# Retention: who masks the second eight heads' scores

## The reference, cut to what matters

```
scores = einsum('bhld,bhmd->bhlm', q, k) * D[None]      # D[h, n, m] = gamma_h ** (n - m), 0 above the diagonal
ret    = einsum('bhlm,bhmd->bhld', scores, v)
ret    = (ret * silu(xo)) @ reto_w + reto_b
x      = x + ret
```

## Time and profile before

| | us |
|---|---|
| median of 3 runs | 1049.51 |
| lowest and highest | 1049.19, 1051.26 |
| profiled execution, its own time | 1046.18 |
| profiled execution, span of the trace | 1044.3 |
| DVE busy | 602.1 (58%) |
| ACT busy | 331.3 (32%) |
| POOL busy | 329.7 (32%) |
| PE busy | 702.2 (67%) |

### The profile page before, as it was taken

The page is one execution under the profiler, slowest core; times in us unless marked ns, Lnnn a source line. Parts: engine busy times, 40 slices in busy tenths (PEclk is TensorE's granted clock), DMA queues, the critical chain, the costliest instruction groups (busy, mean ns, idle before and its releaser), DMA issues. The chain is left out here.

```text
span 1044.3 us, 19748 instructions
## 1 busy us (share of the span) xinstructions
PE 702.2 (67%) x6652; PEld 477.3 (46%) x6652; DVE 602.1 (58%) x1825; ACT 331.3 (32%) x565; POOL 329.7 (32%) x654
## 2 busy tenths in 40 slices
PE   1789887889883119997215398378569863089991
PEld 0355455555562018996111144234234432078991
DVE  7978545889288706664504376246347527146763
ACT  2232324333421014442320156145245541034440
POOL 0123300134331756776430001101100115746771
PEclk9899998999975559999555599779779985589996
DMA  9101595111200115553321101101100000145554
GB/s 225 43 26 57 118 190 123 42 42 42 56 1 10 47 50 154 159 166 112 112 107 71 53 3 47 82 11 42 79 17 3 3 1 32 51 119 150 156 162 133
DMA packets 99569, 80.89 MB, mean 77 GB/s; under 512 B 7383, under 2 KB 91418, under 8 KB 98730
## 3 DMA queue, kind: packets, MB, share of 16 engines
q1 hardware_dynamic: 94926, 70.25, 24.9%
q0 software_dynamic: 4544, 9.38, 2.7%
HBM read 54.44 MB, written 23.40 MB: 75 GB/s over the span
## 5 line engine op out<-in xcount | busy, mean ns | idle before, releaser
L1153 DVE TENSOR_REDUCE rmax<-PA 128x1 f32<-128x512 f32 (+3 forms) x256 | 120.9, 490 | 151.1 <-PE PA L1791 143.3
L728 POOL DMA_INDIRECT outs_dram<-va,ids x78 | 93.8, 1202 | 54.8 <-POOL ids L724 27.8
L1086 DVE SCALAR_TENSOR_TENSOR pm<-PB,invb,decay 128x512 f32<-128x512 f32 x78 | 58.1, 744 | 61.9 <-ACT decay L1400 61.9
L1751 PE MATMUL PC<-ffn_w,pm 128*128 128x128 f32 x624 | 88.0, 284 | 6.9 <-DMA ffn_w<-in_w 4.8
L1789 PE MATMUL PA<-mqb,idb 128*128 128x128 bf16 x256 | 60.6, 238 | 45.1 <-DMA qst<-qst 29.9
L1791 PE MATMUL PA<-kst,qst 96*128 96x512 bf16 (+3 forms) x256 | 84.5, 336 | 0.0
L1751 PEld LDWEIGHTS PC<-ffn_w,pm 128*128 128x128 f32 x624 | 75.7, 191 | 11.1 <-DMA ffn_w<-in_w 7.2
L1392 ACT ACTIVATE kv_b<-P 128x256 f16<-128x256 f16 x78 | 29.9, 383 | 156.3 <-PE P L1730 152.2
L713 POOL DMA_INDIRECT rows_dram<-va,idx x64 | 64.4, 1006 | 45.7 <-DVE va L1039 26.8
L1467 ACT ACTIVATE pm<-PB 128x1024 f32<-128x1024 f32 (+1 forms) x64 | 44.9, 702 | 101.9 <-PE PB L1814 101.8
L1789 PEld LDWEIGHTS PA<-mqb,idb 128*128 128x128 bf16 x256 | 25.5, 100 | 107.6 <-issue 58.2
(11 more groups left out here) (214 smaller groups left out, 1585.4 us busy)
## 6 DMA issues: line engine op xcount, KB each, us to landing
ffn_w<-in_w SPq DMA_DIRECT2D x78, 256.0 KB
rows_dram<-wall SPq DMA_DIRECT2D x1, 8385.0 KB, 46.3
X<-in_w SPq DMA_DIRECT2D x32, 256.0 KB, 2.9
proj_w<-rows_dram SPq DMA_DIRECT2D x78, 65.0 KB
qst<-parts_dram SPq DMA_DIRECT2D x12, 384.0 KB
kst<-parts_dram SPq DMA_DIRECT2D x12, 384.0 KB
X<-in_x SPq DMA_DIRECT2D x8, 256.0 KB, 4.8
R<-outs_dram SPq DMA_DIRECT2D x4, 512.0 KB, 3.8
```

The costliest lines, as they stand in the source:

```text
L728: nc.gpsimd.indirect_dma_start(out=outs_dram, out_offset=bass.IndirectOffsetOnAxis(ap=ids[:, k % YB:k % YB + 1], axis=0), in_=ysb[:, k % Y ...
L1086: nc.vector.scalar_tensor_tensor(out=eT[:, k % 2, :, :].rearrange("p f n -> p (f n)"), in0=PB[:, k % 2, :], scalar=invb[:, k % 2:k % 2 + 1 ...
L1153: nc.vector.tensor_reduce(rmax[:, i, h % HG:h % HG + 1], PA[:, n % 2, 0:(i + 1) * P], AX_X, ALU.max).then_inc(pair_sb[n % 2], 1)
L1751: ins = mm(PC[:, k % 2, 0:D], eT[:, k % 2, f, :], w2b[k % WB2][:, f, :], start=f == 0, stop=f == FB - 1)
```

## The change

The masking of heads 8 to 15 is taken from VectorE and done in two steps. ScalarE copies the raw scores from PB into the second half of `pm` (`raw_scores`), and GpSimd multiplies them there, in place, with the decay (`decay_half`). Two semaphores are new, `raw_sb` and `pm2_sb`; `pm_sb` now counts one per tile. TensorE's next scores wait for VectorE's masking of PA and for ScalarE's copy; its retention product waits for VectorE and for GpSimd. On ScalarE the four copies of a group stand between the other work: one before the Silu, one behind it, and one behind each of the two high halves' places. On GpSimd the product stands behind `decay_k` and ahead of `norm_factors`.

```
+            def decay_half(g):
+                pool.wait_ge(raw_sb, g + 1)
+                nc.gpsimd.tensor_tensor(pm[:, 2 * (g % 2) + 1, :], pm[:, 2 * (g % 2) + 1, :],
+                                        decay[:, H // 2:H, :].rearrange("p h n -> p (h n)"),
+                                        ALU.mult).then_inc(pm2_sb, 1)
...
+            pool.wait_ge(in_decay, 16)
             for layer in range(LAYERS):
                 for t in range(NT):
                     decay_k(layer * NT + t)
+                    decay_half(layer * NT + t)
                     if t % TPS == 2 and t > TPS:
                         norm_factors(layer * SEQ + t // TPS - 1)
...
-                        decay_scores(t, 0)
+                        decay_scores(t)
                     if t >= 2:
                         add_out(t - 2)
-                    if t < NT:
-                        decay_scores(t, 1)
...
+                def raw_scores(t):
+                    g = layer * NT + t
+                    act.wait_ge(sc_ps, 2 * g + 2)
+                    if g >= 2:
+                        act.wait_ge(re_ps, g - 1)
+                    nc.scalar.activation(pm[:, 2 * (g % 2) + 1, :], PB[:, :, :].rearrange("p b n -> p (b n)"),
+                                         ACT.Copy).then_inc(raw_sb, 1)
...
+                    raw_scores(TPS * s)
                     nc.scalar.activation(sxT[:, c % 2, :], ring("xo", layer, s), ACT.Silu,
                                          bias=proj_bc[:, layer, 3:4]).then_inc(ring_sb, 1)
+                    raw_scores(TPS * s + 1)
                     if layer == 1:
                         high_weight(2 * s)
+                    raw_scores(TPS * s + 2)
+                    if layer == 1:
                         high_weight(2 * s + 1)
+                    raw_scores(TPS * s + 3)
                     if s >= 1:
                         normalize(2 + 2 * layer, s - 1)
...
                     if g >= 1:
-                        pe.wait_ge(pm_sb, 2 * g)
+                        pe.wait_ge(pm_sb, g)
+                        pe.wait_ge(raw_sb, g)
...
-                    pe.wait_ge(pm_sb, 2 * g + 2)
+                    pe.wait_ge(pm_sb, g + 1)
+                    pe.wait_ge(pm2_sb, g + 1)
```

More of the change, by code:

```diff
@@ L429, in mixer_kernel @@
         pm_sb = sem("pm_sb")
+        raw_sb = sem("raw_sb")
+        pm2_sb = sem("pm2_sb")
         re_ps = sem("re_ps")
@@ L867, in decay_q, with decay_scores @@
                         bc(const[:, C_GQ:C_GQ + P], [P, TPS, P], 1), ALU.mult).then_inc(qg_sb, 1)
-                def decay_scores(t, u):
+                def decay_scores(t):
                     g = layer * NT + t
[L871 to L875, removed]
+                    dve.wait_ge(sc_ps, 2 * g + 1)
+                    nc.vector.tensor_tensor(pm[:, 2 * (g % 2), :], PA[:, :, :].rearrange("p b n -> p (b n)"),
+                                            decay[:, 0:H // 2, :].rearrange("p h n -> p (h n)"),
                                             ALU.mult).then_inc(pm_sb, 1)
@@ L1702, in down @@
                     ins.then_inc(f2_ps, 1)
-                pe.wait_ge(pm_sb, 2 * NT * (layer + 1))
+                pe.wait_ge(pm2_sb, NT * (layer + 1))
                 pe.wait_ge(ro_up, NT * (layer + 1))
```

## The result

The changed kernel takes 1064.12 us (median of 4 runs, 1058.39 to 1065.81); the kernel before 1050.38 in its own 4. One of those four took 1125.42 us, in a slower state that the chip is sometimes in, and the ratio leaves it out; the other three have a median of 1049.51. The ratio is 1.0125, 95% interval 1.0079 to 1.0172: slower by some 13 us. The forecast was 1064.3. It stood at 315.2 us before and stands at 329.2: +13.9. (The whole span is longer by only 12.3; where the last 1.6 came back was not examined.)

What follows compares the result with a forecast made beforehand. VectorE, or TensorE, sets the pace, with GpSimd's chain on the path entering tiles 8 and 12. Layers' +4.7 and +10.1 us make 1046.18 into 1061.0; 3.3 for the runs' median gives 1064.3, range 1053 to 1072 (8 in 10).

Steps and rivals of the forecast that it cites:

- the hold: In both retention stages, VectorE instructions with two SBUF operands (state updates, decay_q, layer 1's low_weight) wait behind GpSimd's 2.36 us product.
- The walk: All engine queues followed tile by tile through both retention stages: +4.7 us in layer 0, +10.1 in layer 1, +14.8 in sum.
- the port: GpSimd instructions and VectorE ones with two SBUF inputs exclude each other; the walk without this gave +5.0 us.
- the late chain: At the entry to tiles 8 and 12, GpSimd's product delays norm factors, normalising, evacuation and TensorE's projections; alone +5.0 us.
- rival 1: No mutual holding of GpSimd and VectorE, only the chain late: +1.9 and +3.1 us, 1052 to 1054.5; chance 0.12.
- Layer 0, tiles 0 to 5, +0.7: Tile 0's retention product waits for GpSimd, which ends 2.5 us later than VectorE's second half did: +0.7 us.
- Entry to tile 12, "+2.36 again": Layer 0: tile 10's product again precedes the chain, +2.36 us; VectorE having won back 1 us, lateness is +3.5.
- Rival 3: TensorE's clock also falls behind the idle gaps before tiles 8 and 12 in each layer: +6.8 us, 1071; chance 0.10.
- Layer 0 should lose half of what layer 1 loses: Sign across the two layers: forecast +4.7 and +10.1 us; equal losses would say the weights' halves have no part.
- If the time from tile 4 to tile 8 is not 24 to 26 us in both layers, the walk is wrong: Sign to check the walk: time between the maskings in tiles 4 and 8, expected 24 to 26 us in both layers.
- Rival 2: TensorE becomes the bound and VectorE's relief shows; the four groups shrink by up to 7 us: 1042.5; chance 0.06.
- rival 4: The change moves nothing because TensorE's work covers both: within 2 us of 1049.5; chance 0.04.

Runs made afterwards that it cites:

- both layers filled: The changed kernel with small idle TensorE products before the fourth group's query projection and the last retention in each layer; 1.0040 of the kernel before.
- norm factors first: The kernel before, with GpSimd's norm factors moved ahead of decay_k in tiles 6, 10 and 14; 0.9985 of the kernel before.
- The fills: The changed kernel with GpSimd's product replaced by three scratch fills, together as long, reading nothing from SBUF; 1.0093 of the kernel before.
- the layer 1 run: The changed kernel with small idle products filling TensorE's gaps in layer 1 only; 1.0075 of the kernel before, the change beside it 1.0113.
- the hybrid: The changed kernel with ScalarE and GpSimd masking only in each group's first two tiles, VectorE in the others; 1046.45 us, 0.9932 of the kernel before.
- the copy-only kernel: The changed kernel with ScalarE's copy kept but VectorE, not GpSimd, multiplying the copied scores in SBUF; 1.0022 of the kernel before.
- half the product: The changed kernel with GpSimd's product covering 512 of 1024 numbers, four heads keeping raw scores; 0.9973 of the kernel before.

## Why the prediction was right, and where it was wrong

The sign was right, and so were the durations, the places of the waits and the hold as such. That the number was right to 0.2 us is luck: the forecast put the hold too high by some 6 us and the clock at nothing, where it is 6 to 8.

**Durations, places, the hold: right.** The product at 2.36 us and not 2.13; the copy at 1.02; no table load; `decay_k`, product, norm factors, normalising, evacuation, projections in that order, with a gap of 3.40 us for "3 to 4". The norm factors of tile 6 end at 74.2, not 75.6, since the product could start at 67.2 and not 68.65. A held state update of 2.23 us and low halves up to 2.2 (I had said up to 3). The estimate of 2.25 from the Trainium skill (GPSIMD Engine Reference, "Elementwise — side-by-side cycle accounting") was 5% low against the trace's 2.357; the figure of that page is for an add, where I had written product.

**The walk against the profiles.** Lateness in us against the kernel before, counted in each layer from its first masking:

| | forecast | the change | both layers filled |
|---|---|---|---|
| layer 0, tile 4 | +0.7 | -0.8 | 0.0 |
| layer 0, tile 8 | +2.2 | +2.5 | +1.7 |
| layer 0, tile 12 | +3.5 | +2.1 | +2.5 |
| layer 0, last sum | +4.7 | +2.1 | +1.4 |
| layer 1, tile 8 | +3.6 | +3.6 | +2.2 |
| layer 1, tile 13 | +6.0 | +3.8 | +3.7 |
| layer 1, last sum | +10.1 | +9.9 | +7.1 |

The last column is nearest to the waits alone, which is what the forecast added up. Its sum at the FFN end is +7.7. The kernel before has a half-speed stretch, some 1.6 us by the run with its norm factors first, and the filled kernel one of 0.8; with both taken off the waits are 7.7 + 1.6 - 0.8 = 8.5 us, where the forecast had 14.8.

**The step that was sized wrong: what the hold costs.** The prediction's own walk without the port gave +5.0, so 14.8 holds 9.8 us for the hold. The fills, without it, are 3.0 us faster than the change by the ratios, and about 4 earlier at the FFN end by the estimate above. Taken off 8.5 that leaves some 5 us for the late chain alone, an estimate, as rival 1 had it. So the hold was put too high by about 6 us, and the chain about right. In the table it shows most in the second half of layer 1, where the low halves of the weights are held: from tile 8 to the last sum the filled kernel loses 4.9 us, where I had 10.1 - 3.6 = 6.5, and tile 13 stands at +3.7 for +6.0. Why a held instruction costs less there than walked was not tested.

**Layer 0, tiles 0 to 5, +0.7: wrong sign.** The rows of the change show why.

```profile
38.73 1.21 DVE L883 TENSOR_TENSOR pm<-PA,decay 128x1024 f32<-128x1024 f32 x1
39.87 0.41 DVE L867 TENSOR_TENSOR vs<-PC,kv_b 128x256 f32<-128x256 f32 x1
41.22 1.23 DVE L883 TENSOR_TENSOR pm<-PA,decay 128x1024 f32<-128x1024 f32 x1 [0.94 <-PE PB L1631]
```

Tile 1's masking comes 2.5 us behind tile 0's; it was 3.65 before, when TensorE waited for VectorE's second masking before it could start tile 1's scores:

```profile
41.04 0.70 PE L1610 MATMUL PA<-kst,qkp 32*128 32x512 f32 x2 [1.66 <-DVE pm L873]
```

The wait that the prediction named is there, tile 0's retention product stands idle for 1.01 us until GpSimd is done, but VectorE's relief is worth more. (In the change's first profile tile 4 of layer 1 is also earlier, by 0.5 us; in the two later ones it is 0.1 and 0.3 later.)

**Entry to tile 12, "+2.36 again": no new wait.** TensorE has no gap of 0.9 us or more there in either layer, and between tiles 8 and 12 the change loses nothing.

**Rival 3, the clock: it got 0.10 and 6.8 us, and it was there.** Measured are 6.2 to 7.7 us by the filled gaps, and 7 to 8.5 with the filled kernel's own slow stretch taken off. Two of the four gaps are those that it named, in front of tile 8; tile 12 has none, and the other two are in front of each layer's last retention. Against it I had put that the fall of before stands where TensorE is busy without a break, but TensorE had been idle for 1.25 us just ahead of it, until 109.17; and that a slow stretch would lie partly in the idle time, but it came behind, when TensorE worked. So rival 3's mechanism held, while its total of 1071 failed, for the waits under it were smaller. That the parts add up to the measured +13.9 to +15.5 (8.5, and 7 to 8.5 for the clock, less 1.6 for the stretch of before) is so by construction; the independent check is the layer 1 run, 4.4 us of them with one layer filled.

**"Layer 0 should lose half of what layer 1 loses":** from the first masking of a layer to the last sum it lost 2.1 and 9.9 us, a fifth. The slow stretch of before lay in layer 0, and the low halves in layer 1; with both layers filled and that stretch added back it is 3.0 and 7.1, nearer to half. **"If the time from tile 4 to tile 8 is not 24 to 26 us in both layers, the walk is wrong":** it was 26.1 and 26.9, so by its own sign the walk was wrong. With the gaps filled it is 24.5 and 25.2: what it lacked there is the clock.

**Rivals 1, 2 and 4** fell by their totals; of rival 1 the price of the late chain fits. Rival 2 has a core of truth, which the hybrid shows: relief of VectorE is worth a few us (7 by the ratio) as soon as GpSimd isn't on the path.

## What to carry to other kernels

An engine that is busy a quarter of the time may still have no slack at a certain place in its queue. Before work is moved to it, find where others wait for it, and put the work where they don't: half of the moved products made this kernel faster, all of them slower. A wait that opens a gap of some 3 us on TensorE may cost twice, in the gap and in the clock behind it; filling the gap with idle products is a cheap test of which it is. And a total that comes out right doesn't show that its terms are: compare the walk with the profile place by place.

## What the runs showed of the hardware

In the change's three profiles each of the four gaps of TensorE of 2.8 to 3.4 us went with half speed (it begins within 1.5 us of the gap's end, behind it or just ahead); products in the gap, 2.84 us of them in front of tile 8, prevented it. No length of gap tells by itself whether the clock falls. Of the gaps of 0.9 to 1.3 us inside the layers of the change's first profile one was followed by half speed, the 1.21 us until 253.84 (0.72 over 254 to 260), and the others weren't; in the copy-only kernel all three of 1.37 us were (0.51 over 68 to 71, 0.50 over 92 to 95, 0.57 over 112 to 115); in half the product those of 2.25 and 2.44 us were, and in the hybrid one of 0.88.

A GpSimd product of 2.36 us holds a state update on VectorE to its end, 2.23 us instead of 0.34; GpSimd fills of the same total length don't hold it, 0.356 us at most. The masking of PA, which reads PSUM and SBUF, is never held in the change (1.226 us at most in 32).
